# First feed-forward of a four-layer kernel: the turn back of a tile one step later, VectorE's largest value first, another order for the last eight tiles, silu one step later

## The reference

```python
def _L0_ffn_ref(x, w1, conv_w, conv_b, w2):
    h = bit_linear(x, w1)                       # 256 -> 1024
    h = depthwise_conv1d(h.transpose(0, 2, 1), conv_w, conv_b)   # 3 taps along the tokens
    h = h.transpose(0, 2, 1)
    h = jax.nn.silu(h)
    return bit_linear(h, w2)                    # 1024 -> 256
...
x = x + jnp.tanh(g_ffn[0]) * _L0_ffn_ref(_layernorm(x, axis=-1), L0_ffn_w1, L0_ffn_conv_w, L0_ffn_conv_b, L0_ffn_w2)
```

## Time and profile before

| | |
|---|---|
| median of 3 runs | 1902.67 us (1902.49 to 1902.95) |
| the profiled execution | 1903.29 us, of which its span 1901.5 us |
| granted TensorE clock, mean | 0.946 |
| PE | 1641.6 us busy, 86% of the span |
| DVE | 1162.2 us, 61% |
| ACT | 882.7 us, 46% |
| POOL | 321.7 us, 17% |
| 250 to 400 us: PE busy, granted clock | 133.64 of 150 us, 1.00 |
| `up`, L372 | 126.1 us for 256 matmuls |

### The profile page before, as it was taken

How to read it: one execution, slowest core, us unless ns; L and a number is a source line. 1 busy time by engine, 2 the same in 40 slices (tenths; PEclk the granted TensorE clock), 3 DMA queues, 4 the chain that set the end, 5 groups by cost and what they waited for, 6 DMA issues and landing times. The chain is left out here.

```text
span 1901.5 us, 29604 instructions
## 1 busy us (share of the span) xinstructions
PE 1641.6 (86%) x10149; PEld 1246.9 (66%) x10149; DVE 1162.2 (61%) x2598; ACT 882.7 (46%) x1795; POOL 321.7 (17%) x359
## 2 busy tenths in 40 slices
PE   7797788887899898799997489999945999989998
PEld 5453345556667666688885279999934888864446
DVE  4668577766456667888986823322247989862116
ACT  2332577664432221466553355555544565533213
POOL 0000000000000101111100345555552111101110
PEclk9898899998899999999998689999977999989999
DMA  6000000003000000100004912222253000000002
GB/s 201 1 1 1 1 1 1 1 1 127 1 1 1 1 1 1 31 2 1 2 1 155 333 59 70 73 71 73 71 191 89 1 1 2 1 1 0 0 1 89
DMA packets 62849, 78.83 MB, mean 41 GB/s; under 512 B 13179, under 2 KB 52655, under 8 KB 62319
## 3 DMA queue, kind: packets, MB, share of 16 engines
q1 hardware_dynamic: 43927, 48.14, 7.5%
q0 software_dynamic: 7584, 20.72, 3.5%
q10 hardware_dynamic: 11192, 8.06, 1.3%
HBM read 58.16 MB, written 18.74 MB: 40 GB/s over the span
## 5 line engine op out<-in xcount | busy, mean ns | idle before, releaser
L2994 PEld LDWEIGHTS moe_bank<-moe_xt,moe_w1e 128*128 128x128 f32 x1264 | 155.0, 193 | 5.8 <-DVE moe_xt L2842 1.8
L2994 PE MATMUL moe_bank<-moe_xt,moe_w1e 128*128 128x128 f32 x1264 | 155.8, 277 | 1.1 <-DVE moe_xt L2842 1.1
L3004 PE MATMUL moe_bank<-moe_w,moe_xin 128*128 x632 | 149.3, 379 | 0.0
L3068 ACT ACTIVATE moe_xin<-moe_bank,moe_b 128x128 f32<-128x128 f32 x316 | 90.3, 368 | 125.1 <-PE moe_bank L2994 125.0
L372 PE MATMUL l0f_hb<-l0f_xt,f_w 128*128 128x512 f32 x256 | 126.1, 625 | 5.3 <-DVE l0f_a L306 3.8
L1471 POOL TENSOR_TENSOR all_x<-all_x,l1x_fbias 128x256 f32<-128x256 f32 x32 | 23.3, 732 | 594.2 <-DVE l1x_fxn L204 594.2
L3004 PEld LDWEIGHTS moe_bank<-moe_w,moe_xin 128*128 128x128 f32 x632 | 114.0, 190 | 12.3
L209 DVE BATCH_NORM_STATS2 all_stats<-all_x 128x6 f32<-128x256 f32 x256 | 104.0, 421 | 5.2
L2851 DVE TENSOR_TENSOR moe_y<-moe_bank,moe_b2r 128x256 f32<-128x256 f32 x79 | 33.5, 424 | 118.8 <-PE moe_bank L3004 118.8
L2911 POOL DMA_INDIRECT moe_results<-moe_y,moe_row x79 | 78.0, 988 | 125.2 <-DVE moe_y L2851 121.9
L2842 DVE COPY moe_xt<-moe_bank 128x256 f32<-128x256 f32 x79 | 33.5, 425 | 106.7 <-PE moe_bank L2982 106.7
(11 more groups left out here) (484 smaller groups left out, 3807.5 us busy)
## 6 DMA issues: line engine op xcount, KB each, us to landing
moe_w<-in_L_ffn_W SPq DMA_DIRECT2D x32, 512.0 KB, 10.4
moe_w<-moe_results SPq DMA_DIRECT2D x16, 512.0 KB, 8.8
all_x<-in_x SPq DMA_DIRECT2D x4, 1024.0 KB, 12.5
out_x<-all_x SPq DMA_DIRECT2D x8, 512.0 KB
f_w<-in_L_ffn_w_T SPq DMA_DIRECT2D x2, 1024.0 KB, 13.7
moe_inputs<-moe_xin ACTq DMA_DIRECT2D x8, 256.0 KB, 7.5
moe_inputs<-moe_w1e ACTq DMA_DIRECT2D x8, 256.0 KB, 7.8
moe_b2r<-in_L_ffn_b SPq DMA_DIRECT2D x1, 2048.0 KB, 14.2
```

Of the source, the lines that this page charges most:

```text
L2994: ins = nc.tensor.matmul(out, w1e[:, at:at + P], xt[:, u, c * P:(c + 1) * P], start=(c == 0), stop=(c == DC - 1))
L3004: ins = nc.tensor.matmul(bank[4 + u][:, 0:D], ht[:, u, c * P:(c + 1) * P], w2[:, ds(e * (HC * D) + c * D, D)], start=(c == 0), stop=(c == ...
L3068: ins = nc.scalar.activation(ht[:, u, m * P:(m + 1) * P], bank[1 + u][:, m * P:(m + 1) * P], ACT.Gelu, bias=b1[:, ds(e * HC + m, 1)])
```

## The change

In the loop body, `turn_back`, `copy_q` and `down` are those of tile `t - 2` instead of `t - 1`, `quantise` and `largest_hidden` those of `t - 1` instead of `t`, `update` and `stats` those of `t - 3` instead of `t - 2`; `turn_z` stays with tile `t`. So the loops are one slot longer. `zq` gets a second pair of buffers, and `quantise(t)` waits for `turn_back(t - 2)` instead of `(t - 1)`.

TensorE: `turn_z` goes from the middle of the slot to its end, behind `down`; in slots whose `t` is above 24 it stands ahead of `down` and behind both halves of `turn_back`. VectorE: `largest_hidden` goes from behind conv and `dequantise` to the head of the slot. ScalarE: `centre` goes to the head, `silu` handles block `g - 2` instead of `g - 1` and stands right behind it; then come `quantise_x`, the first `copy_q`, both `quantise`, the second `copy_q`, `norm`, `copy_x`. In slots whose `t` is above 24 both `copy_q` stand ahead of `quantise`. The threshold `turn_x` waits for moves with the tile that is turned back.

```diff
--- before.py
+++ after.py
@@ -233,7 +233,7 @@
         xt = s.sb("xt", [P, 2, DC, S])
         a = s.sb("a", [P, 3, S])
         z = s.sb("z", [P, RING, S])
-        zq = s.sb("zq", [P, 2, HM * P])
+        zq = s.sb("zq", [P, 2, 2, HM * P])
         q2 = s.sb("q2", [P, 2, M, P], BF16)
         silu_in = s.sb("silu_in", [P, M])
         hb = [s.ps(f"hb{k}", [P, S]) for k in range(2)]
@@ -325,25 +325,25 @@
                     dve.wait_ge(s.x_ready, t + 1)
                     tile_stats(nc, sh, t).then_inc(s.stats_ready, 1)
 
-                for g in range(END + 3):
+                for g in range(END + 4):
                     t = g - LAG
                     b, m = g // M, g % M
-                    if 0 <= t - 2 < T:
-                        update(t - 2)
+                    if 0 <= t - 1 < T:
+                        largest_hidden(t - 1)
+                    if 0 <= t - 3 < T:
+                        update(t - 3)
                     if 1 <= g <= SLOTS:
                         conv(g - 1, 0)
                         conv(g - 1, 1)
                     if b < B - 1 and m >= HM:
                         dequantise((b + 1) * TB + 2 * (m - HM))
                         dequantise((b + 1) * TB + 2 * (m - HM) + 1)
-                    if 0 <= t < T:
-                        largest_hidden(t)
                     if b < B - 1 and m < HM:
                         largest_input(b + 1, 2 * m, 2)
                         if m == HM - 1:
                             input_scales(b + 1)
-                    if 0 <= t - 2 < T:
-                        stats(t - 2)
+                    if 0 <= t - 3 < T:
+                        stats(t - 3)
                     if g == 2:
                         dve.wait_ge(s.w2_scaled, 1)
                         c.link(nc.vector.tensor_scalar(w2[:, :, :], w2[:, :, :], MAGIC, 1.0, ALU.subtract, ALU.min))
@@ -399,7 +399,7 @@
                     else:
                         pe.wait_ge(s.q2_ready, 2 * (t - 1) + half + 1)
                     for i in range(HM):
-                        ins = nc.tensor.transpose(back_bank(t, half)[:, i * P:(i + 1) * P], zq[:, half, i * P:(i + 1) * P], sh.ident[:, :])
+                        ins = nc.tensor.transpose(back_bank(t, half)[:, i * P:(i + 1) * P], zq[:, t % 2, half, i * P:(i + 1) * P], sh.ident[:, :])
                     ins.then_inc(s.back_ps, 1)
 
                 def down(t):
@@ -417,28 +417,27 @@
                 for t in range(0, TB, 2):
                     turn_x(t, 0)
                 fed = TB
-                for g in range(END + 2):
+                for g in range(END + 3):
                     t = g - LAG
                     b, m = g // M, g % M
-                    if t > TAIL and t < T:
-                        turn_z(t, 0)
-                        turn_z(t, 1)
-                    if 0 <= t - 1 < T:
-                        turn_back(t - 1, 0, fed)
+                    if 0 <= t - 2 < T:
+                        turn_back(t - 2, 0, fed)
                     if g < SLOTS:
                         up(g, 0)
-                    if 0 <= t - 1 < T:
-                        turn_back(t - 1, 1, fed)
-                    if 0 <= t <= TAIL:
-                        turn_z(t, 0)
-                        turn_z(t, 1)
+                    if 0 <= t - 2 < T:
+                        turn_back(t - 2, 1, fed)
                     if g < SLOTS:
                         up(g, 1)
                     if b < B - 1 and m >= HM:
-                        turn_x(fed, max(0, 2 * t))
+                        turn_x(fed, max(0, 2 * (t - 1)))
                         fed += 2
-                    if 0 <= t - 1 < T:
-                        down(t - 1)
+                    if 0 <= t - 2 < T and t <= TAIL:
+                        down(t - 2)
+                    if 0 <= t < T:
+                        turn_z(t, 0)
+                        turn_z(t, 1)
+                    if t > TAIL and t - 2 < T:
+                        down(t - 2)
 
             @block.scalar
             def _(act):
@@ -478,9 +477,9 @@
 
                 def quantise(t, half):
                     act.wait_ge(s.sc2_ready, t + 1)
-                    if t:
-                        act.wait_ge(s.back_ps, 2 * (t - 1) + half + 1)
-                    nc.scalar.activation(zq[:, half, :], z_bank(t)[:, half * HM * P:(half + 1) * HM * P], ACT.Copy, bias=MAGIC,
+                    if t >= 2:
+                        act.wait_ge(s.back_ps, 2 * (t - 2) + half + 1)
+                    nc.scalar.activation(zq[:, t % 2, half, :], z_bank(t)[:, half * HM * P:(half + 1) * HM * P], ACT.Copy, bias=MAGIC,
                                          scale=sc2[:, t:t + 1]).then_inc(s.zq_ready, 1)
 
                 def copy_q(t, half):
@@ -498,25 +497,28 @@
                 nc.scalar.activation(silu_in[:, :], cb[:, :], ACT.Silu).then_inc(s.table_loaded, 1)
                 act.wait_ge(s.table_loaded, 1)
                 nc.scalar.activation(w2[:, :, :], w2[:, :, :], ACT.Copy, bias=MAGIC, scale=wscale[:, 1:2]).then_inc(s.w2_scaled, 1)
-                for g in range(END + 2):
+                for g in range(END + 3):
                     t = g - LAG
                     b, m = g // M, g % M
+                    if 1 <= g <= SLOTS:
+                        centre(g - 1)
+                    if 2 <= g <= SLOTS + 1:
+                        silu(g - 2)
                     if b < B - 1 and m >= HM:
                         quantise_x((b + 1) * TB + 2 * (m - HM))
                         quantise_x((b + 1) * TB + 2 * (m - HM) + 1)
-                    if 1 <= g <= SLOTS:
-                        centre(g - 1)
+                    if 0 <= t - 2 < T:
+                        copy_q(t - 2, 0)
+                        if t > TAIL:
+                            copy_q(t - 2, 1)
                     if 0 <= t - 1 < T:
-                        copy_q(t - 1, 0)
-                        copy_q(t - 1, 1)
+                        quantise(t - 1, 0)
+                        quantise(t - 1, 1)
+                    if 0 <= t - 2 < T and t <= TAIL:
+                        copy_q(t - 2, 1)
                     if b < B - 1 and m < HM:
                         norm((b + 1) * TB + 2 * m)
                         norm((b + 1) * TB + 2 * m + 1)
-                    if 1 <= g <= SLOTS:
-                        silu(g - 1)
-                    if 0 <= t < T:
-                        quantise(t, 0)
-                        quantise(t, 1)
                     if b < B - 1 and m >= HM:
                         copy_x((b + 1) * TB + 2 * (m - HM))
 
```

## The result

The changed kernel takes 1876.32 us in the median of 4 runs (1874.90 to 1881.07) against 1902.81 of the kernel before: a ratio of 0.9866, 95% interval [0.9849, 0.9882]. That is 26.5 us less. Forecast were 21.5 less, 1881, in a range of 1874 to 1893. The profiled execution took 1876.34 us for a span of 1874.6.

The account below looks back on a forecast made before the run. Bound: a circle of ScalarE and VectorE in slots without x work, also holding copy_x and quantise_x in those with it. Terms -1.2 - 2.9 - 6.9 - 9.5 - 2.7 - 4.5 = -27.7, +6.2 for clock: -21.5, 1881 us, range 1874 to 1893.

Parts of the forecast that it names:

- rival 1: Whole kernel: TensorE's clock stays up, so the gain is 27.7 us, 1875; chance 0.16.
- the clock's term: TensorE falling to its low clock at slots 4, 8, 9, 33 and 34 takes back 6.2 us of the gain.
- A slots: Slots without x work: 6.13 us, TensorE's own need, instead of 6.54; -1.2 in slots 16 to 19.
- B slots: Slots with x work, batches 1 and 2: VectorE's order makes a new circle, 7.69 us instead of 8.60; -6.9.
- Slots 1 to 11: silu stops waiting for its slot's conv, quantise_x leaves the circle: -9.5 up to slot 10, -2.7 in slots 10 and 11.
- Tail: Slot 32 to last down: slots 32 and 33 wait for the second copy, later slots take 2.74 us; -4.5.
- Start to start on VectorE: B slots: counting hand-offs from recorded ends would cut the gain by 1.4 us; the forecast used the trace's earlier starts.
- Rival 2: Hand-offs left out keep B slots at 8.5 us and the tail near 3.4 a tile: 1892.6; chance 0.25.
- Rival 3: Whole kernel: the order does nothing, the same semaphores bind in another place: 1902.7; chance 0.04.
- Rival 4: The clock falls within slots 12 to 31 too, making the kernel slower: over 1906.5, or 1918; chance 0.05.

Follow-up runs that it names:

- e4: The changed kernel with dequantise ahead of the convolution pair on VectorE: 1865.94 us.
- e9: The kernel before with only the two quantise_x moved behind centre: 1893.40 us.
- e3: The changed kernel with the last tiles in the order of the rest (down ahead of turn_z, second copy_q behind quantise): 1904.06 us.
- e2: The changed kernel with silu handling block g - 1 behind norm again: 1880.63 us.
- e10: e4 with quantise_x behind the first copy_q instead of ahead of it: 1863.91 us.
- e7: The kernel before with only silu one step later and right behind centre: 1909.07 us.
- e1: The changed kernel with largest_hidden back behind the convolution pair and dequantise on VectorE: 1922.67 us.
- e6: The changed kernel with 14 added transposes into an unread bank ahead of down in slots 32 and 33: 1876.53 us.

## Why the prediction was right, point by point

The direction, the mechanism and nearly all sizes held. The time came out 4.7 us below the forecast and 1.3 above rival 1's 1875, so it lies only 0.3 inside the forecast's own 1876 to 1887. What separates forecast and rival 1 is the clock's term, and there the trace lies about midway.

- **A slots.** Right that ScalarE and VectorE stop being the bound and TensorE becomes it. The slot is 6.06, not 6.13: in the slot whose length I took the earlier trace rows the steps behind the two halves of `turn_back` start 0.48 and 0.46 later (303.05 and 305.25 in the trace); now it is 0.44 and 0.43. That is -0.8 over twelve slots that I left out.
- **B slots.** 7.70 against 7.69, and e4 shows the circle to be the real one. What the prediction didn't say is how little of this needs the whole change: `quantise_x` behind `centre` alone gives 7.56 in the kernel before (e9), so in B slots the rest of the change puts one circle in another's place and gains nothing more.
- **Slots 1 to 11.** -10.4 against -9.5 with the clock, so right in size. At full clock the first part was to take 59.44 - 9.5 = 49.9 us, and e3, whose clock nearly held there, took 49.8 with the same code. The reasons were silu and `quantise_x` together, as the prediction has them. Slot 4's `turn_x` comes 3.5 us earlier, counted from the first `up`, and 2.5 of it go when silu is put back (e2). From there to slot 7's `turn_x` the place of `quantise_x` brings 0.8 a slot (5.72 instead of 6.51), with the old silu too. It was the expectation of e2, with 6 us, that gave silu too much.
- **Tail.** The walk was right: slots 32 and 33 wait for the second copy 1.78 us each, then 2.74 a tile; without a fall of the clock it takes 35.61 against 35.64 (e10). e3 shows that this order is worth some 28 us, which the prediction had not priced.
- **The clock.** The step that was mis-sized. I took 6.2 us of losses; the trace has 0 at slot 4, some 1.6 in slots 8 and 9 (16 matmuls in 8.67 us where two times 3.44 and the last one's 0.15 would be 7.0) and 1.3 in slot 33. That is 2.9, so 3.3 too much. With the A slots' 0.8, and 0.2 the other way in the B slots, that is the distance of the stretches, 25.3 against 21.5; the 0.9 that is left to the 4.7 is within the scatter. I put every place where TensorE idled long at the low level for the whole of the work behind it; in slot 33 only one `down` and some 0.6 of a `turn_z` were hit, `turn_back` and slot 34 no more. How much falls is in part luck of the execution: with the same code the loss in slots 8 and 9 was 1.6 us in one trace and 0.5 in another (e3), and with the same idle times that in the tail 1.3 and nothing (e10). The Trainium skill, "TensorE: Matmul & The Clock Gate", section "HAM oscillation — how this bites in real kernels", says that bursts with waits between them start cold again and again; e3 comes near that (clock 0.74 over its tail), the changed kernel shows it in slots 8, 9 and 33 only. The page's waits are DMA waits of 3 to 5 us, those here 0.7 to 2.7.
- **Start to start on VectorE.** The rule that an operation waits for the whole of the one ahead (the Trainium skill, "VectorE: DVE Perf Modes", section "The DRAIN you can't avoid", which adds that one that is not held starts earlier) would have made a B slot 0.17 longer, if recorded ends are meant. `dequantise` started 0.08 before conv's recorded end again (second pass at 264.03 for 1.28, so 265.31, against 265.23), and the slot came out at 7.70: the rows carry the sum.
- **Rivals.** Rival 2 (hand-offs left out) didn't occur: no wait appeared that the walk hadn't named. Rival 3 and 4 neither. Rival 4's mechanism, waits that take the clock along until the gain is gone, is real, however: it is e3, if in the tail and not in slots 12 to 31.

Not settled: why the clock held at slot 4 (it fell there in the kernel before, in e2 and in e9: 5.37 us for eight matmuls), in e10's tail and nearly so in e3's slots 8 and 9, while the same or like idle times brought it down elsewhere. One profile for each kernel can't tell.

## What to carry to other kernels

With queues in order, draw the circle that the steps of one period form across engines and add its start-to-start times; a move pays only if it takes something out of that circle, and the same move (silu behind centre) gained 3 us in one arrangement (e2) and cost 9 in another (e7). Delaying a stage by one tile gained nothing (e3), or cost 20 us (e1), until the consumer's queue order and the end of the loop were changed with it. In the last slots, where no other work fills the waits, look at the order anew: it decided some 28 of 1876 us here. And where an effect of 1 or 2 us is read from one profile, look first whether the clock did the same in both (e4, e6, e10).

## What the hardware showed that I hadn't expected

The waits of a bad tail can cost more than their own length, since they take the clock along: 6.8 to 7.1 us a tile instead of 5.5 (e3), granted clock 0.74. TensorE's clock is not settled by the code alone: one and the same stretch of code ran 16 matmuls in 8.67 us in one trace and in 7.50 in another (e3), and the same waits of the tail went with 0.58 in one and 1.00 in another (e10). With 1.7 us of work that nobody reads in the waits of 1.78 it read 1.00 as well (e6), and the tail was 1.3 us shorter; that the work was the cause is not shown.
